# Batch attention on Trainium2: values from one product per group and a DRAM spread, output from one product

## The reference, cut to what matters

```python
S, B, H = (32, 256, 128)          # after the earlier layers; 16 heads of 8
xn = layernorm(x, ln1_w, ln1_b)
q, k, v = split(xn @ in_proj_w.T + in_proj_b)
scores = q @ k^T / sqrt(8), causal along the 32 tokens   # per position and head
attn = softmax(scores) @ v
x1 = x + attn @ out_proj_w.T + out_proj_b
```

## Time and profile before

| | |
|---|---|
| median of 3 runs | 2315.8 us (2306.62 to 2316.9) |
| profiled execution | 2328.56 us |
| its span, first to last instruction | 2326.8 us |
| PE busy | 1911.3 us (82%) |
| DVE busy | 1481.1 us (64%) |
| ACT busy | 1306.2 us (56%) |
| POOL busy | 1061.4 us (46%) |
| mean granted clock of TensorE | 0.918 |

### The profile page before, as it was taken

The page is one execution under the profiler, slowest core; times in us unless marked ns, Lnnn a source line. Parts: engine busy times, 40 slices in busy tenths (PEclk is TensorE's granted clock), DMA queues, the critical chain, the costliest instruction groups (busy, mean ns, idle before and its releaser), DMA issues. The chain is left out here.

```text
span 2326.8 us, 52990 instructions
## 1 busy us (share of the span) xinstructions
PE 1911.3 (82%) x16969; PEld 1587.6 (68%) x17001; DVE 1481.1 (64%) x5945; ACT 1306.2 (56%) x3148; POOL 1061.4 (46%) x1320
## 2 busy tenths in 40 slices
PE   7799999999999788788866888859999983676764
PEld 6555555555555677788864777748999973676764
DVE  2477788888788558332116999848878868343334
ACT  3588888888887342334334888844545530254443
POOL 2133333333333311555547888643556561355554
PEclk9899999999999798899997999979999985688787
DMA  7799999999999300445551222230010016444441
GB/s 227 268 311 316 312 306 317 315 307 318 314 308 311 114 37 7 131 143 153 155 138 31 55 60 60 50 75 1 2 19 19 2 19 92 125 140 127 126 132 49
DMA packets 191613, 348.54 MB, mean 150 GB/s; under 512 B 24530, under 2 KB 140250, under 8 KB 190832
## 3 DMA queue, kind: packets, MB, share of 16 engines
q1 hardware_dynamic: 154384, 300.12, 40.8%
q0 software_dynamic: 16304, 34.74, 6.4%
q10 hardware_dynamic: 20656, 10.29, 1.5%
HBM read 160.19 MB, written 142.25 MB: 130 GB/s over the span
## 5 line engine op out<-in xcount | busy, mean ns | idle before, releaser
L182 POOL TENSOR_SCALAR_AFFINE_SELECT heads_raw_relative<-heads_raw_relative 128x508 f32<-128x508 f32 x256 | 166.7, 675 | 498.3 <-ACT heads_raw_relative L567 458.2
L567 ACT COPY heads_raw_relative<-heads_rel_bank 128x768 f32<-128x768 f32 x247 | 198.6, 804 | 121.9 <-PE heads_rel_bank L462 121.7
L491 PE MATMUL attend_turn_bank<-ident,attend_score 128*128 128x128 f32 x1536 | 230.7, 286 | 21.3 <-ACT attend_prob_t L573 20.0
L491 PEld LDWEIGHTS attend_turn_bank<-ident,attend_score 128*128 128x128 f32 x1536 | 163.2, 141 | 117.3 <-ACT attend_prob_t L573 68.8
L573 ACT ACTIVATE attend_prob_t<-attend_turn_bank 128x384 f32<-128x384 f32 x512 | 224.8, 500 | 6.2 <-PE attend_turn_bank L491 6.2
L577 ACT ACTIVATE attend_score<-attend_score,attend_extreme 128x128 f32<-128x128 f32 x512 | 215.7, 421 | 9.1 <-DVE attend_extreme L624 8.8
L624 DVE CUSTOM_DVE_ANT_0 attend_score<-attend_score_bank,heads_relative 128x256 f32<-128x256 f32 x512 | 214.7, 419 | 0.0
L1396 POOL DMA_INDIRECT moe_route_rows_sb<-tokens,moe_taken x154 | 146.0, 948 | 125.3 <-PE moe_route_bank L1418 81.9
L630 DVE TENSOR_SCALAR attend_score<-attend_score,attend_extreme 128x256 f32<-128x256 f32 x512 | 195.4, 382 | 0.0
L621 DVE CUSTOM_DVE_ANT_0 attend_score<-attend_score_bank,heads_relative 128x128 f32<-128x128 f32 x512 | 146.6, 286 | 73.6 <-PE attend_score_bank L462 48.9
L1881 PE MATMUL duo_hid_bank<-duo_rows_t,duo_w_now 128*128 128x128 f32 x728 | 121.9, 321 | 83.7 <-ACT duo_rows_t L1915 75.6
(11 more groups left out here) (414 smaller groups left out, 5610.8 us busy)
## 6 DMA issues: line engine op xcount, KB each, us to landing
shear<-heads_raw_relative SPq DMA_DIRECT2D x128, 768.0 KB
heads_relative<-shear SPq DMA_DIRECT2D x128, 768.0 KB
duo_w_now<-moe_w SPq DMA_DIRECT2D x182, 129.0 KB
moe_route_w_now<-moe_w SPq DMA_DIRECT2D x154, 129.0 KB
expert_out<-moe_route_y ACTq DMA_DIRECT2D x38, 256.0 KB
qk_heads<-heads_qk_out SPq DMA_DIRECT2D x32, 256.0 KB, 4.5
heads_qk<-qk_heads SPq DMA_DIRECT2D x128, 64.0 KB
pair_rows<-groups SPq DMA_DIRECT2D x16, 260.0 KB, 8.8
```

The costliest lines, as they stand in the source:

```text
L182: m = nc.gpsimd.affine_select(out=future, in_=future, compare_op=ALU.is_ge, fill=-BIG, base=1 - P, pattern=[[0, QUAD], [1, P - 1]], channe ...
L491: mm = nc.tensor.transpose(bank[:, j * P:(j + 1) * P], score[:, (h - LAG) % RING, j * P:(j + 1) * P], c.ident[:, :])
L567: nc.scalar.copy(raw[:, ring, 2 * half:2 * half + 2, :], r_bank[:, :, 0:W]).then_inc(rel_moved, 1)
```

## The change

Values. The rows are no longer copied per block. `value(f)` makes one product per group for a whole step, tokens on partitions and features on columns, right behind `project` in s1 of the step before. ACT's `values_out` copies them to `v_rows`. SP stores these to DRAM (`c.values`) and reads them back with four transfers, one per block a, each taking 32 features of all tokens to the 32 partitions of its block (`v_near`). POOL's `place_values`, in s0 and s1 of the step itself, multiplies each half with `of_a` into `v_blocks` of all four groups, and orders the columns by digit b first. `mix` waits for both halves of its step.

Output. With digit b first, the features of digit b lie on one quarter of the partitions of `o_bank`. ACT's `outputs_out` copies four quadrants, each with its own columns, into one [128, 4, 32] tile, and `output(g)` is one product with `w_out`. The masked weights and `column_a` go. The rows that SP sends out per 16 groups now stand behind the value transfers in its queue, and the loads of the experts' weights behind the first of them.

```diff
@@ Core: one more DRAM tensor @@
+        self.values = dr("batch_values", [2, P, 4, D])
@@ BatchConstants: column_a and its two affine_selects go (made counts 8 instead of 11) @@
@@ attend_batches: tiles @@
-        w_out_b = sb("w_out_b", [P, HB, D])
-        v_blocks = [sb(f"v_blocks{s}", [P, NPG, D]) for s in range(SLOTS)]
+        v_rows = sb("v_rows", [P, SLOTS, D])
+        v_blocks = [sb(f"v_blocks{v}", [P, SLOTS * NPG, D]) for v in range(2)]
+        v_near = sb("v_near", [P, SLOTS * NPG, P // HB])
-        prob_t, out_t = sb("prob_t", [P, NPG * P]), sb("out_t", [P, HB, NPG, B])
+        prob_t, out_t = sb("prob_t", [P, NPG * P]), sb("out_t", [P, NPG, B])
@@ SyncE @@
+            def spread_values(f):
+                v = f % 2
+                sp.wait_ge(v_out, f + 1)
+                sp.dma_start(c.values[v], v_rows[:, :, :]).then_inc(v_stored, 16)
+                sp.wait_ge(v_stored, 16 * (f + 1))
+                wait_past(sp, v_placed, 2 * f)
+                rows = c.values[v].rearrange("(n s) g d -> s g n d", n=NPG)
+                for x in range(HB):
+                    at, wide = slice(B * x, B * (x + 1)), slice(P // HB * x, P // HB * (x + 1))
+                    sp.dma_start(v_near[at, :, :].rearrange("p (g n) d -> p g n d", g=SLOTS), rows[:, :, :, wide]
+                                 ).then_inc(v_in, 16)
+            spread_values(0)
             sp.dma_start(ex.w1[:, :, 0:H2], ex.w1_dram.rearrange("e c h -> c e h")).then_inc(experts_in, 16)
...
+            for f in range(1, STEPS):
+                spread_values(f)
+                if f % SLOTS == SLOTS - 1 and f > SLOTS:
+                    send_rows(f // SLOTS - 1)
+            send_rows(STEPS // SLOTS - 1)
@@ GpSimd @@
-            def spread(f, v):
...
-                nc.gpsimd.tensor_copy(hn_blocks[v][:, :, :, :], rows).then_inc(hn_spread, 1)
+            def place_values(f, half):
+                v = f % 2
+                pool.wait_ge(v_in, 16 * HB * (f + 1))
+                wait_past(pool, o_made, SLOTS * (f - 1))
+                at = slice(SLOTS * NPG // 2 * half, SLOTS * NPG // 2 * (half + 1))
+                wide = [P, SLOTS * NPG // 2 * HB, HB, HD]
+                near = v_near[:, at, :].rearrange("p g (b c) -> p (g b) c", c=HD).unsqueeze(2).broadcast_to(wide)
+                of_block = of_a[:, :].unsqueeze(1).unsqueeze(3).broadcast_to(wide)
+                nc.gpsimd.tensor_tensor(v_blocks[v][:, at, :].rearrange("p g (b a c) -> p (g b) a c", a=HB, b=HB), near, of_block,
+                                        ALU.mult).then_inc(v_placed, 1)
...
                     normalise_probs(g, s % 2)
-                    if s == 1 and not last:
-                        spread(f + 1, 1 - v)
+                    if s < 2:
+                        place_values(f, s)
@@ TensorE @@
-            def value(g, s, v):
-                pe.wait_ge(v_ready, g)
-                for n in range(NPG):
-                    rows = hn_blocks[v][:, s * NPG + n, :, :].rearrange("p h s -> p (h s)")
-                    mm = nc.tensor.matmul(v_bank[:, n * D:(n + 1) * D], rows, w_in[:, 2 * D:],
-                                          start=True, stop=True)
+            def value(f, v):
+                wait_past(pe, v_out, f)
+                for s in range(SLOTS):
+                    mm = nc.tensor.matmul(v_bank[:, s * D:(s + 1) * D], positions(hn[v], s), w_in[:, 2 * D:], start=True, stop=True)
                 mm.then_inc(v_made, 1)
...
+            def mix(g):
+                f, s = g // SLOTS, g % SLOTS
                 pe.wait_ge(p_out, g + 1)
                 pe.wait_ge(o_out, g)
+                pe.wait_ge(v_placed, 2 * f + 2)
...
-                for b in range(HB):
-                    mm = nc.tensor.matmul(x_bank[:, 0:D], out_t[:, b, :, :].rearrange("p n s -> p (n s)"), w_out_b[:, b, :],
-                                          start=b == 0, stop=b == HB - 1)
+                mm = nc.tensor.matmul(x_bank[:, 0:D], out_t[:, :, :].rearrange("p n s -> p (n s)"), w_out[:, :], start=True, stop=True)
...
-                    value(g, s, v)
...
                             project(f + 1, 1 - v)
+                            value(f + 1, 1 - v)
@@ ScalarE @@
-                nc.scalar.copy(out_t[:, :, :, :], o_bank[:, :].rearrange("p (n h s) -> p h n s", n=NPG, h=HB)
-                               ).then_inc(o_out, 1)
+                for b in range(HB):
+                    at = slice(P // HB * b, P // HB * (b + 1))
+                    x = nc.scalar.copy(out_t[at, :, :], o_bank[at, :].rearrange("p (n h s) -> p n h s", n=NPG, h=HB)[:, :, b, :])
+                x.then_inc(o_out, 1)
+            def values_out(f):
+                act.wait_ge(v_made, f + 1)
+                wait_past(act, v_stored, 16 * f)
+                nc.scalar.copy(v_rows[:, :, :].rearrange("p g d -> p (g d)"), v_bank[:, :]).then_inc(v_out, 1)
...
                             place_queries(f + 1, 1 - v)
+                            values_out(f + 1)
@@ VectorE @@
-            for b in range(HB):
-                nc.vector.tensor_scalar(w_out_b[:, b, :], w_out[:, :], of_b[:, b:b + 1], None, ALU.mult)
...
-            def place_values(g, s):
-                dve.wait_ge(v_made, g + 1)
-                nc.vector.tensor_tensor(v_blocks[s][:, :, :], v_bank[:, :].rearrange("p (n d) -> p n d", d=D),
-                                        along(column_a[:, :, :].rearrange("p h d -> p (h d)"), NPG), ALU.mult
-                                        ).then_inc(v_ready, 1)
...
-                    place_values(g, s)
@@ host layout: the columns of the value bias and the rows of out_proj_t are reordered, second digit of the head first @@
```

More of the change, by code:

```diff
@@ L2575, in attend_batches @@
         hn = [sb(f"hn{v}", [P, C]) for v in range(2)]
-        q_blocks, k_blocks, hn_blocks = ([sb(f"{x}{v}", [P, SLOTS * NPG, HB, B]) for v in range(2)]
-                                         for x in ("q_blocks", "k_blocks", "hn_blocks"))
-        v_blocks = [sb(f"v_blocks{s}", [P, NPG, D]) for s in range(SLOTS)]
+        q_blocks, k_blocks = ([sb(f"{x}{v}", [P, SLOTS * NPG, HB, B]) for v in range(2)]
+                                         for x in ("q_blocks", "k_blocks"))
+        v_rows = sb("v_rows", [P, SLOTS, D])
+        v_blocks = [sb(f"v_blocks{v}", [P, SLOTS * NPG, D]) for v in range(2)]
+        v_near = sb("v_near", [P, SLOTS * NPG, P // HB])
         centred, e_x, prob = ([sb(f"{x}{u}", [P, NPG * HB, B]) for u in range(2)] for x in ("centred", "e_x", "prob"))
@@ L2619, in _, with send_rows @@
                              ).then_inc(experts_in, 16)
-            for k in range(NT // PART):
+            def send_rows(k):
                 sp.wait_ge(rows_normed, (k + 1) * PART // SLOTS)
@@ L2679, in step @@
                         normalise_rows(f - 2, 1)
-            spread(0, 0)
+            pool.wait_ge(made, 8)
             step(0, 0, first=True)
@@ L2768, in turn_probs @@
                 mm.then_inc(p_turned, 1)
-            def mix(g, s):
+            def mix(g):
+                f, s = g // SLOTS, g % SLOTS
                 pe.wait_ge(p_out, g + 1)
                 pe.wait_ge(o_out, g)
+                pe.wait_ge(v_placed, 2 * f + 2)
                 for n in range(NPG):
-                    mm = nc.tensor.matmul(o_bank[:, n * P:(n + 1) * P], v_blocks[s][:, n, :], prob_t[:, n * P:(n + 1) * P],
+                    mm = nc.tensor.matmul(o_bank[:, n * P:(n + 1) * P], v_blocks[f % 2][:, s * NPG + n, :], prob_t[:, n * P:(n + 1) * P],
                                           start=True, stop=True)
@@ L2811, in step @@
                     if back:
-                        mix(g - 2, (s - 2) % SLOTS)
+                        mix(g - 2)
                     if not first or s >= 3:
@@ L2817, in _ @@
             project(0, 0)
+            value(0, 0)
             step(0, 0, first=True)
@@ L2825, in _ @@
                 turn_probs(NT - 2 + s, s)
-                mix(NT - 2 + s, SLOTS - 2 + s)
+                mix(NT - 2 + s)
                 output(NT - 3 + s)
@@ L3063, with by_second_digit @@
     column = lambda name: take(name)[:, None]
+    def by_second_digit(rows):
+        values = rows[2].reshape(4, 4, HD).swapaxes(0, 1).reshape(D)
+        return _np.stack([rows[0], rows[1], values], axis=1)
     laid_out = {
```

32 lines of the change are left out of this document (10 added, 22 removed).

## The result

The changed kernel takes 2322.97 us (median of 20 runs, 2308.31 to 2336.14) against 2317.5 us before (20 runs, 2306.62 to 2324.34); the ratio is 1.0028, 95% interval 1.0015 to 1.0041. So it is 0.3% slower, less than the 0.5% that the prediction counts as a difference, and the time lies 3 us from the 2320 predicted. The profiled execution took 2308.31 us, the fastest of the 20; its span is 2306.2 us, at a mean clock of 0.914.

What follows compares the result with a forecast made beforehand. The prediction took the PE, DVE, POOL, PE hand-over in s2, the third slot, as the bound. Steps +1 us (-1.3 +1.4 each, 15 steps), start +6, end -2 gave +5 on 2315.8, so 2320 us; range 2296 to 2345.

Steps and rivals of the forecast that it cites:

- PE's part: Per attention step, merged value products save 2.67 us and merged output products 2.68; PE's work falls from 20.4 to 15.05 us.
- DVE's part: Per attention step, four place_values of 0.68 us go; DVE's work falls from 18.1 to about 15.7 us.
- ACT's part: Four quadrant copies take 0.8 us (bounds 0.59 and 1.06) against 0.59; ACT's step rises from 10.5 to about 12, hidden.
- POOL's part: Two masks of 2.0 us each (1.9 to 2.4) per step; the second, behind s1's normalisation, holds up the mix of s0.
- The walk: Waits traced slot by slot round one attention step: 19.2 us against 20.5, saving 1.3 us, with PE standing still 3.1 us.
- The clock: PE's 3.1 us pause lowers the granted clock in four steps of five, 1.7 us each, costing 1.4 us per step.
- Start: At the attention stage's start the values' way isn't hidden: +6 us, bounds +3 to +9.
- the values' way through DRAM: Store 4.5 us plus gather 7.3, 11.8 us in all; hidden within 16 us in steady steps, exposed at the start.
- the forecast's row of 2308 to 2331: Main case: the pause comes, the clock falls in 8 to 15 of 15 steps, mask 1.9 to 2.2 us; chance 0.44.
- the clock that holds: Rival: PE's pause brings no fall of the clock; -15.5 us, 2300 us, or 2296 with a cheaper mask and start; chance 0.28.
- a mask over 2.5 us: Rival: POOL's mask is dearer, lengthening the pause in s2; 2343 us at a mask of 3.5 us; chance 0.18.
- a gather over 11.5 us: Rival: the values' way exceeds 16 us and POOL's queue stands; a gather of 12.5 us gives 2335 us; chance 0.08.

Runs made afterwards that it cites:

- e1: Changed kernel with both of POOL's masks of a step made one behind the other in s0, the first slot; ratio to the kernel before 0.9886.
- e2: Changed kernel with twelve unused 128x128 products on PE filling its pause before the mix of s0, the first slot; ratio to the kernel before 0.9939.
- e3: Kernel before with the output part of the change alone, values as before; ratio to the kernel before 0.9876.
- e13: e8 with the bias added to four groups of rows once per step, then one addition per slot with a PSUM input; ratio to the kernel before 0.9825.
- e8: e7 with ACT's copy of the next values moved from s1 to s2, the third slot; ratio to the kernel before 0.9878.
- e9: Changed kernel with only DVE's preparation of the next rows moved from s1 to s0, the first slot; ratio to the kernel before 0.9969.
- e7: e1 with DVE's preparation of the next rows also moved from s1 to s0; ratio to the kernel before 0.9867.
- e5: Changed kernel with each mask over half its positions from the third step on, so values are incomplete; ratio to the kernel before 0.9899.
- e4: Changed kernel with the output as before, so the values part of the change alone; ratio to the kernel before 1.0132.
- e10: e8 with DVE's addition of the output rows moved behind the next slot's sums and reciprocal; ratio to the kernel before 1.0005.
- e12: e3 with DVE's addition of the output rows moved behind the next slot's sums and reciprocal; ratio to the kernel before 1.0055.

## Why the prediction was right, point by point

Both mechanisms of the prediction are shown: the second mask ends PE's pause (e1 moves it, and the pause goes from 3.1 to 1.3 us), and the pause brings the fall of the clock (e2 fills it, and the clock stays). That the time came out within 3 us is in part luck. The sum gave +5 us, and the medians differ by 5.5, but in the two profiles the terms of the stage are +3.7 for the fourteen steps, -3.85 for the step with the experts' bias, +2.6 at the start and -2.3 at the end, 0.2 in all. What the remaining 5 us are isn't shown. Term by term:

- **PE's part.** 2.67 and 2.68 us per step were to go. e3 alone saved 1.3 of its 2.68, where DVE became the bound. e13 shows a step of 15.67 busy us at full clock against the 15.05 of the prediction.
- **DVE's part.** Forecast 15.7 us of a step; 17.30 measured, of which 1.9 are the stall of the preparation.
- **ACT's part.** The quadrants took 1.04 to 1.06 us for four (255 ns each) where I took 0.8, at the bound of 1.06. What PE waited for was the mask all the same. No run has shorter quadrants; e8 shows only that ACT's copy of the values isn't on the path with the masks moved, and in e1 and e13 PE's pause ends with ACT's copy of the probabilities.
- **POOL's part.** The mask took 1.89 us; I took 2.0 with 1.9 as the end. The straight line through the earlier trace rows (1.92) was nearly exact. The estimate from the Trainium skill (GPSIMD Engine Reference, section 3.1), 2.2 us, was further off; the measurement decides.
- **The walk.** It gave 19.2 us for a step without the fall of the clock. The changed kernel's two such steps took 19.18 and 19.05; the mean of the fourteen less 1.4 us for the falls is 19.2. By slots, from s3: 4.34, 3.10, 5.57, 6.19 forecast, 4.47, 3.26, 5.37, 6.08 in the step of 19.18. So the walk was right, in s1 to s2 by luck: it has no stall of DVE in s1 to s2, and e9, without the stall and with the preparation elsewhere, takes 4.8 us there. I had charged DVE's rows addition with nothing, and in the steady part rightly (median 292 ns in the earlier trace rows and after); but the preparation in s1 I never set beside the mask, and it went from 0.28 to 0.7 us each. e9 prices this at 0.25 us per step. The cost of a meeting, "up to 0.8", was too low: the addition of rows lost 1.4 us to the masks in e7.
- **The clock.** Four steps of five and 1.7 us each, 1.4 per step, was forecast. It fell in 12 of 14 and cost 1.4 per step by the two steps without a fall (at least 0.8 by e2). So the count and the cost were both near right. Net: -1.1 + 1.4 = +0.3 us per step in place of -1.3 + 1.4 = +0.1.
- **The step with the experts' bias** was not looked at. It went from 27.35 to 23.50 us, 3.9 us that the sum doesn't have. No run was made for its cause.
- **Start.** Forecast +6, measured +2.6: from DVE's first instruction of the stage to the fourth centred 26.65 us before and 29.27 after. The term that was mis-sized is the values' way through DRAM: 11.8 us in the prediction, but 2.0 us from the store's issue to the gather's, and at most 5.9 from there to the first mask, which was then waiting for the normalisation ahead of it. Four transfers of 512 pieces of 512 B were a poor bound for as many of 128 B. In the steady part POOL never waited for `v_near`.
- **End.** Forecast -2, measured -2.3 (last centred to the stage's end).

By its own terms the forecast's row of 2308 to 2331 comes out at about 2312 to 2329 (8 falls and a mask of 1.9; 15 falls and one of 2.2), which changes nothing in the outcome. Of the rivals, that of the clock that holds (0.28) rested on the earlier trace rows, that a pause of 2.30 us did no harm. e5 shows falls after 7 of 12 pauses of 1.90 us, so it had less for it than I thought. The slower ones, a mask over 2.5 us and a gather over 11.5 us, were both off by a wide margin. The question that the prediction didn't ask is whether the two parts of the change belong together: e3 and e4 answer that they don't, as long as the second mask stands where it does. Of the better kernels, e3 (0.9876) is as fast as e8 (0.9878), which has the values' part and three moves more; only e13 (0.9825) shows the values' part worth having, and no run has e13's addition on top of e3.

## What to carry to other kernels

When work moves to another engine's queue, its place in the queue can outweigh its length: here 1.89 us of mask behind the wrong instruction cost more than 5.35 us of PE's work gained, and one moved line turned 1.0028 into 0.9886. Write, for the engine that takes the work, which instructions of its neighbour will lie beside it: in these kernels DVE's additions of two SBUF tensors (0.29 to 1.66 us) and its SBUF to SBUF products (0.28 to 1.87) stood still while GpSimd ran a two-input product, so give such an addition an input from PSUM or a place where GpSimd has none. A reordering that is meant to remove one such meeting must be walked through all slots, for it can make three others (e10 and e12).

## What the runs showed of the hardware

The stall is the finding I had not expected in its size. Counted over the fourteen traces (before, after and the twelve runs), by what POOL was already running, with at least 0.06 us to go, when DVE's instruction began (times are medians in us unless said):

| DVE instruction, 128x128 unless said | beside POOL's one-input products | beside its two-input products |
|---|---|---|
| rows, two SBUF inputs | 243 of them, 0.292; twenty of these 0.34 to 0.51, and two in e3 1.37, where a groups addition came next | mask 37, 1.66; normalisation 155, 1.16; groups 23, 0.89 |
| preparation, SBUF to SBUF | 225, 0.28; some longer, to 0.53 | mask 95, 1.87; groups 11, 1.12; normalisation 38, 0.29, begun in its last third |
| fresh, one input from PSUM | 286, 0.28 | 95, at most 0.294 |
| e13's rows, one input from PSUM | 16, 0.28 | 24, at most 0.292 |
| total, a sum over 128x512 of SBUF | 261, at most 0.689 | 88, at most 0.689 |

The stalled instruction ends 0.08 us (preparation) or 0.15 us (rows) after POOL's: it waits out what is left of it. The Trainium skill (SBUF — State Buffer, section "Who interferes with whom") tells of one pair of SBUF ports that VectorE and GpSimd share and hold for a whole instruction, taken by VectorE's two-port modes, which `tensor_scalar` can enter, and, its read side alone, by its instructions with two SBUF inputs. The traces agree with that in the right-hand column, and in that sums never wait. In the left-hand one they agree in part at most: the section has two SBUF inputs contend with any GpSimd instruction that reads SBUF, and the second to come wait for the first to finish, but the 243 additions of rows beside POOL's one-input products kept a median of 0.292 us, and the twenty longer ones ended 0.21 us before POOL's instruction did.

Two smaller ones. A copy from PSUM of a quadrant of 32 partitions by 128 takes ACT 255 ns, nearly that of 128 partitions by 128 (265 ns); four of them cost 1.05 us, against 0.59 for the one copy they replace. And after pauses of PE of about equal length the clock fell in some steps and not in others (1.90 us: 7 of 12 in e5; 1.50 to 2.19 us: 2 of 14 in e13).
